# A pre-norm transformer block on one core: the key block that two query tiles share is weighed with split products, and head and tail are reordered

## The chip, the cores and the metric

The kernel runs on one core of a Trainium2 chip. The metric is the device time of one execution in microseconds, the median of the runs shown. TensorE (PE) does the matrix products and is the only writer of the eight PSUM banks; VectorE (DVE) and ScalarE (ACT) read and write SBUF and PSUM; GpSimd (POOL) reads and writes SBUF only here; SyncE (SP) issues all the DMAs. Each engine works through its own instructions in order, and they meet at semaphores.

## The reference

A transformer block on x of 1024 tokens by 256, in float32: layernorm without weights, attention with 16 heads of 128 over a window of 128 keys, a residual, layernorm again, a feed-forward of 1024 with ternary weights and an exact gelu, a residual.

```python
q, k, v = split_heads(h @ wq), split_heads(h @ wk), split_heads(h @ wv)
q, k = _apply_rotary(q, cos, sin), _apply_rotary(k, cos, sin)
valid = (k_pos > q_pos - WINDOW) & (k_pos <= q_pos)
attn = softmax(where(valid, einsum('bhqd,bhkd->bhqk', q, k) * scale, neg))
x = x + concat_heads(einsum('bhqk,bhkd->bhqd', attn, v)) @ wo
# then, on layernorm(x), w1q and w2q being weights rounded to -1, 0, 1:
x = x + einsum('bsf,df->bsd', gelu(einsum('bsd,fd->bsf', h, w1q) + b1), w2q) + b2
```

## The kernel before

**Split products.** Most products run in a one-pass format (`F32R`) on operands that are split in two: a high part, which is the value rounded by a copy into that format, and a low part, which is the value minus the high part. A product of two split operands is three passes: hi by lo, lo by hi, hi by hi. The exception is `weigh_v`, which multiplies plain float32 operands; the profile shows each such product as two instructions.

**Tiles and steps.** There are 64 steps, one for each head and each quarter j of the tokens (two query tiles of 128, `t = 2j` and `2j + 1`). A query tile sees two key tiles: its own and the one ahead of it. So step (head, j) has to do with the key tiles 2j - 1, 2j and 2j + 1, and key tile 2j is seen by both query tiles. On TensorE, step n holds `scores(n)` (into bank `SC`), `transpose_probs(n - 1)` (into `PT`), `project(n + 4)` (q or k of a half of the tokens, into `PR`), a fill if there is one, and `weigh_v(n - 1)` (into `OT`). Fills are the projections of v and of the output for quarters of the tokens, `("v", i)` and `("o", i)`, which use the two banks `VO` in turn; steps 2 to 6 have none. `bank_free` waits until the fill before in the same bank has been read. The last eight steps belong to the last two heads and interleave them.

**The way of a step.** DVE `merge(n)` overlays the two masked halves of the scores and takes the negative maximum; ACT `exps(n)` does the exponentials with sums; DVE `inverse_sum(n)` the reciprocals; ACT `scale_probs(n)`; PE transposes; DVE `mask_pt(n - 1)` writes `probsT`, [128, i, b, 128] for query tile i and key tile b (0: the one ahead, 1: its own); PE `weigh_v(n - 1)`; ACT `ot_hi` and DVE `ot_lo` split its result out of `OT`, and the next `weigh_v` waits for that.

**Rotary.** For each projected chunk m, DVE multiplies by sine (`times_sin`) and by cosine (`times_cos`); SP's `swap(m)` sends the sine product through a DMA that swaps the halves of the partitions; `rotate(m)` adds (L949, on POOL; the first two on DVE at L735); ACT's `rothi(m)` (L589) and `rotlo(m)` (L954 on POOL) split it. POOL also makes the low parts of the weights: `qklo` (L936), `vlo` (L940), `olo` (L944), and the first half of the ternary rounding, `below` (L961), in every second step from 25 to 39; the second half, `ternary` (L796), is DVE's, and both `ternary`'s inputs and its output are in SBUF. In POOL's loop over n the order is `rotlo(n + 2)`, `rotate(n + 3)`, then low parts of weights and `below` where they fall.

**Head and tail.** The head normalises x, transposes it, and does the first projections; the order of each engine's instructions there is written out by hand. The tail takes the steps after 60 into the second layernorm (`tile_stats`, `moments`, `normalise`), whose first half starts when half of the outputs have been added to `xres` (`add_out`, L778), and then the feed-forward (`ffn1` L488, gelu, `ghi` and `glo` for the split, `ffn2` L507).

## Time and profile before

| what | value |
|---|---|
| median of 3 runs | 361.02 us (360.62 to 361.49) |
| the profiled execution's own time | 360.54 us |
| its span | 358.8 us |
| mean granted TensorE clock | 0.99 |
| PE, DVE, ACT, POOL busy | 340.5, 263.8, 208.1, 223.5 us |
| DMA packets, volume | 29025, 31.25 MB |

The span runs from the first to the last instruction of the profiled execution. Busy is the time in which an engine has at least one instruction at work; a PE that is busy throughout is not at its peak, as the ends of its products are modelled and overlap the next one. Times from start to start say more for PE. In the rows below, columns are start us, duration us, engine, line, operation, output<-inputs with buffer numbers left out, shape, count, and in brackets the idle time ahead of it and what ended it.

### The profile page before, as it was taken

Reading aid. Unit: us, or ns where it says so; the run is one execution under the profiler, and the core shown is the slowest. Engines: PE = TensorE matmul, PEld = TensorE weight load, DVE = VectorE, ACT = ScalarE, POOL = GpSimd, SP = SyncE. Lnnn points to the kernel's source line nnn. Section 1 sums busy time; section 2 is a strip of 40 time slices with the busy share of each in tenths; the row PEclk is TensorE's granted clock in tenths of the full one; section 3 lists DMA queues with packets and bytes.
Section 4 is the critical chain, followed back from the end, with each engine's and each line's share of the span. In section 5 each row is a group of like instructions: output and inputs, shape, how many; then the busy total and the mean of one; then the engine's idle time right before and its main releaser. Section 6 shows DMA issues by size and latency. Waiting matters only on the chain.

```text
span 358.8 us, 6923 instructions
## 1 busy us (share of the span) xinstructions
PE 340.5 (95%) x2410; PEld 315.1 (88%) x2410; DVE 263.8 (74%) x607; ACT 208.1 (58%) x626; POOL 223.5 (62%) x182
## 2 busy tenths in 40 slices
PE   7849999999999999999999999999999999898996
PEld 6738778999999999999999999999999999877986
DVE  4874777668766886788788986787678766788681
ACT  2243676677777556655665566556665666365180
POOL 2326778667767678799879987585867656231300
PEclk9997999999999999999999999999999999999999
DMA  7734466543333333333333333333322231000001
GB/s 220 188 95 114 117 164 197 130 102 78 92 83 86 80 84 84 88 81 89 88 90 88 90 88 90 90 89 90 88 61 58 61 88 31 0 3 0 31 29 58
DMA packets 29025, 31.25 MB, mean 87 GB/s; under 512 B 3392, under 2 KB 20288, under 8 KB 28992
## 3 DMA queue, kind: packets, MB, share of 16 engines
q1 hardware_dynamic: 28992, 30.82, 33.7%
q8 instruction: 19, 0.31, 0.4%
q14 instruction: 14, 0.11, 0.1%
HBM read 12.98 MB, written 1.05 MB: 39 GB/s over the span
## 4 chain that ended last, share of the span: by engine, by line
PE 84%; DVE 9%; POOL 2%; issue 2%; DMA 1%; ACT 1%; DVEq 0%; SPq 0%; POOLq 0%
PE PR L385 22%; PE OT L460 15%; PE VO L400 13%; PE SC L435 12%; PE VO L417 11%; PE PT L446 3%; PE PR L488 2%; PE SC L488 2%; PE VO L507 1%; DVE probsT L765 1%; PE SC L507 1%; DVE stats L690 1%; DVE SC L751 1%; DVE gT_lo L807 1%; DVE gT_lo L772 1%
## 5 line engine op out<-in xcount | busy, mean ns | idle before, releaser
L954 POOL TENSOR_TENSOR gT_lo<-turn,gT_hi 128x512 fp32r<-128x512 f32 x62 | 81.7, 1318 | 42.9 <-ACT gT_hi L589 42.7
L949 POOL TENSOR_TENSOR turn<-turn,swapped 128x512 f32<-128x512 f32 x62 | 80.2, 1293 | 38.2 <-DMA swapped<-by_sin 37.9
L594 ACT ACTIVATE probs<-SC,negmax 128x128 f32<-128x128 f32 x128 | 45.8, 363 | 61.9 <-DVE negmax L754 61.9
L460 PE MATMUL OT<-probsT,v_sb 128*128 128x128 f32 x480 | 64.6, 276 | 3.1 <-DVE gT_lo L772 2.7
L601 ACT ACTIVATE probs<-probs,rinv 128x128 f32<-128x128 f32 x128 | 44.5, 395 | 38.2 <-DVE rinv L759 38.2
L460 PEld LDWEIGHTS OT<-probsT,v_sb 128*128 128x128 f32 x480 | 58.9, 191 | 6.0 <-DVE probsT L765 6.0
L385 PE MATMUL PR<-xT_hi,qk_lo 128*128 128x512 f32 x128 | 56.2, 439 | 5.1 <-POOL qk_lo L936 3.7
L751 DVE COPY_PREDICATED SC<-in_prev_sb,SC 128x256 f32<-128x256 int32 x48 | 20.6, 428 | 45.7 <-PE SC L435 45.5
L385 PE MATMUL PR<-xT_hi,qk_hi 128*128 128x512 f32 x128 | 51.0, 398 | 0.0
L385 PE MATMUL PR<-xT_lo,qk_hi 128*128 128x512 f32 x128 | 50.4, 394 | 0.0
L765 DVE TENSOR_TENSOR probsT<-PT,mask_sb 128x512 f32<-128x512 f32 x64 | 43.6, 681 | 1.2 <-PE PT L446 1.2
L589 ACT CAST gT_hi<-turn 128x512 fp32r<-128x512 f32 x64 | 38.9, 607 | 8.5 <-POOL turn L949 7.6
L435 PE MATMUL SC<-gT_hi,gT_lo 128*128 128x256 f32 (+1 forms) x128 | 41.1, 321 | 0.4 <-DVE gT_lo L740 0.4
L400 PE MATMUL VO<-v_lo,xT_hi 128*128 128x256 f32 x128 | 36.7, 287 | 1.0 <-POOL v_lo L940 1.0
L417 PE MATMUL VO<-o_lo,gT_hi 128*128 128x256 f32 x128 | 36.3, 284 | 1.0 <-DVE xres L778 1.0
L400 PE MATMUL VO<-v_hi,xT_hi 128*128 128x256 f32 x128 | 36.6, 286 | 0.0
L400 PE MATMUL VO<-v_hi,xT_lo 128*128 128x256 f32 x128 | 36.5, 285 | 0.0
L417 PE MATMUL VO<-o_hi,gT_hi 128*128 128x256 f32 x128 | 36.0, 282 | 0.0
L435 PE MATMUL SC<-gT_lo,gT_hi 128*128 128x256 f32 (+1 forms) x128 | 36.0, 281 | 0.0
L435 PE MATMUL SC<-gT_hi 128*128 128x256 f32 (+1 forms) x128 | 35.9, 281 | 0.0
L417 PE MATMUL VO<-o_hi,gT_lo 128*128 128x256 f32 x128 | 35.9, 281 | 0.0
L385 PEld LDWEIGHTS PR<-xT_hi,qk_lo 128*128 128x128 f32 x128 | 24.3, 190 | 8.5 <-POOL qk_lo L936 3.9
(114 smaller groups left out, 839.1 us busy)
## 6 DMA issues: line engine op xcount, KB each, us to landing
swapped<-by_sin SPq DMA_DIRECT2D x128, 128.0 KB, 2.3
qk_raw<-in_wq SPq DMA_DIRECT2D x16, 128.0 KB, 2.6
qk_raw<-in_wk SPq DMA_DIRECT2D x16, 128.0 KB, 2.4
v_raw<-in_wv SPq DMA_DIRECT2D x8, 256.0 KB, 3.1
o_raw<-in_wo SPq DMA_DIRECT2D x8, 256.0 KB, 2.9
xres<-in_x SPq DMA_DIRECT2D x4, 256.0 KB, 3.2
w_raw<-in_w1t SPq DMA_DIRECT2D x4, 256.0 KB, 3.0
w_raw<-in_w2t SPq DMA_DIRECT2D x4, 256.0 KB, 3.0
```

Source lines behind the costliest of these rows:

```text
L385: last = mm(PR[m % 2][:], wt[:, c % 2, kd], xt[:, kd, half_of(c)], start=(n == 0), stop=(n == 3 * KD - 1))
L400: last = mm(VO[v % 2][:, i * 256:(i + 1) * 256], xt[:, kd, t * P:(t + 1) * P], wt[:, kd], start=(n == 0), stop=(n == 3 * KD - 1))
L417: last = mm(VO[w % 2][:, i * 256:(i + 1) * 256], ot[:, t * P:(t + 1) * P], wt[:, a], start=(n == 0), stop=(n == 5))
L435: last = mm(SC[n % 2][:, o0:(i + 1) * 256], q[:, t * P:(t + 1) * P], k[:, k0 * P:(t + 1) * P], start=(p_ == 0), stop=(p_ == 2))
L460: last = mm(OT[:, i * P:(i + 1) * P], v_sb[:, t - 1 + b, a * HD:(a + 1) * HD], probsT[:, i, b], start=(b == b0), stop=(b == 1))
L589: copy(rot_hi(head, c % 2)[:, half_of(c)], turn[m % 4][:]).then_inc(rothi_done, 1)
L594: nc.scalar.activation(probs[n % 2][:, i], SC[n % 2][:, i * 256 + P:(i + 1) * 256], ACT.Exp, bias=negmax[:, n % 2, i:i + 1], accum_out=row ...
L601: last = nc.scalar.activation(probs[n % 2][:, i], probs[n % 2][:, i], ACT.Copy, scale=rinv[:, n % 2, i:i + 1])
L751: nc.vector.copy_predicated(sc[:, :, 1], in_prev_sb[:].unsqueeze(1).broadcast_to([P, 2, P]), sc[:, :, 0]).then_inc(merged, 1)
L765: tt(probsT[:], PT[:, 0:256].rearrange("p (i q) -> p i q", i=2).unsqueeze(2).broadcast_to([P, 2, 2, P]), mask_sb[:].unsqueeze(1).broadcast ...
L949: tt(turn[m % 4][:], turn[m % 4][:], swapped[m % 2][:], ALU.add).then_inc(rot_done, 1)
L954: tt(rot_lo(head, c % 2)[:, half_of(c)], turn[m % 4][:], rot_hi(head, c % 2)[:, half_of(c)].bitcast(F32), ALU.subtract).then_inc(rotlo_don ...
```

## The change

Three things change together. (1) v is kept in three tensors: the odd key tiles as float32 (`v_odd`), the even ones split (`v_even_hi`, `v_even_lo`). `probsT` for the shared even key tile, 256 adjacent columns, is split by ACT (`pt_hi`) and POOL (`pt_lo`) into `both_hi` and `both_lo`, and `weigh_v` does it with three 256-column `F32R` products in place of two float32 products of 128 columns. The products of the odd tiles stay. `copy_v` becomes two copies, and DVE gets `v_low`. (2) Steps 2 to 5 weigh into the `VO` banks that the fills leave free then. (3) The order of the head and of the tail changes on all five engines; on DVE `moments(1, 0)` moves to the start and `normalise(1, 0)` to the middle of step 62, `times_sin(3)` and `times_cos(3)` behind `merge(0)`, and on PE `fill(n)` now stands behind `transpose_x(1, 0)` in the last step.

```diff
@@ tensors
-        v_sb = sb("v_sb", [P, NT, 2 * HD])
+        both_hi = sb("both_hi", [P, 2 * P], F32R)
+        both_lo = sb("both_lo", [P, 2 * P], F32R)
+        v_odd = sb("v_odd", [P, NT // 2, 2 * HD])
+        v_even_hi = sb("v_even_hi", [P, NT // 2, 2 * HD], F32R)
+        v_even_lo = sb("v_even_lo", [P, NT // 2, 2 * HD], F32R)
...
+        def ot_bank(n):
+            return VO[n % 2] if 2 <= n <= 5 else OT
@@ sync, head
+            load_head(1)
             load_table(1, cos_sb)
-            load_head(1)
-            swap(0)
             sp.dma_start(in_prev_sb[:], in_prev).then_inc(mask_in, 16)
             sp.dma_start(mask_sb[:].rearrange("p b q -> p (b q)"), mask_t).then_inc(mask_in, 16)
+            swap(0)
             swap(1)
-            swap(2)
             sp.wait_ge(qklo_done, 1)
             load_head(2)
+            swap(2)
             swap(3)
@@ tensor
-                    pe.wait_ge(*((v_copied, user[1] + 1) if user[0] == "v" else (wo_added, o_at[user[1]] + 1)))
+                    pe.wait_ge(*((v_split, user[1] + 1) if user[0] == "v" else (wo_added, o_at[user[1]] + 1)))
...
+                if v in (4, 5):
+                    pe.wait_ge(otlo_done, v + 1)
                 bank_free("v", v)
@@ weigh_v
-                pe.wait_ge(pt_masked, n + 1)
-                pe.wait_ge(v_copied, 4 * (head // 2) + j + 1)
-                if n > 0:
-                    pe.wait_ge(otlo_done, n)
-                for i in range(2):
-                    t = 2 * j + i
-                    b0 = 1 if t == 0 else 0
-                    for b in range(b0, 2):
-                        last = mm(OT[:, i * P:(i + 1) * P], v_sb[:, t - 1 + b, a * HD:(a + 1) * HD],
-                                  probsT[:, i, b], start=(b == b0), stop=(b == 1))
+                hs = slice(a * HD, (a + 1) * HD)
+                pe.wait_ge(v_split, 4 * (head // 2) + j + 1)
+                if n in (2, 3):
+                    bank_free("v", n + 2)
+                elif n > 0:
+                    pe.wait_ge(otlo_done, {4: 3, 5: 4, 6: 2}.get(n, n))
+                pe.wait_ge(both_hi_done, n + 1)
+                mm(ot_bank(n)[:, 0:256], v_even_hi[:, j, hs], both_hi[:], start=True, stop=False)
+                mm(ot_bank(n)[:, 0:256], v_even_lo[:, j, hs], both_hi[:], start=False, stop=False)
+                if j > 0:
+                    mm(ot_bank(n)[:, 0:P], v_odd[:, j - 1, hs], probsT[:, 0, 0], start=False, stop=False)
+                mm(ot_bank(n)[:, P:256], v_odd[:, j, hs], probsT[:, 1, 1], start=False, stop=False)
+                pe.wait_ge(both_lo_done, n + 1)
+                last = mm(ot_bank(n)[:, 0:256], v_even_hi[:, j, hs], both_lo[:], start=False, stop=True)
                 last.then_inc(pv_done, 1)
@@ tensor, order
-            project(3)
             for n in range(STEPS):
                 scores(n)
+                if n == 0:
+                    project(3)
+                    fill(0)
...
-                fill(n)
                 if n == STEPS - 1:
                     transpose_x(1, 0)
                 if n > 0:
+                    fill(n)
                     weigh_v(n - 1)
@@ scalar
-                copy(v_sb[:, 2 * c:2 * c + 2], VO[v % 2][:].rearrange("p (t n) -> p t n", t=2)).then_inc(v_copied, 1)
+                copy(v_even_hi[:, c], VO[v % 2][:, 0:256])
+                copy(v_odd[:, c], VO[v % 2][:, 256:512]).then_inc(v_copied, 1)
+
+            def pt_hi(n):
+                act.wait_ge(pt_masked, n + 1)
+                copy(both_hi[:], probsT[:].rearrange("p i b q -> p (i b q)")[:, P:3 * P]).then_inc(both_hi_done, 1)
...
+            qkhi(1)
             copy_v(0)
             xt_hi(0, 1)
+            rothi(0)
+            rothi(1)
             copy_v(1)
-            rothi(0)
-            qkhi(1)
-            rothi(1)
-            rothi(2)
...
+                if n == STEPS - 1:
+                    xt_hi(1, 0)
                 exps(n)
                 if n == STEPS - 1:
-                    xt_hi(1, 0)
+                    pt_hi(n - 1)
                     ot_hi(n - 1)
                     nc.scalar.preload_act_table(ACT.Gelu)
                 if n > 0:
+                    if n < STEPS - 1:
+                        pt_hi(n - 1)
...
                 scale_probs(n)
+                if n == 0:
+                    rothi(2)
...
                 if k == 1:
+                    pt_hi(STEPS - 1)
                     ot_hi(STEPS - 1)
@@ vector
+            def v_low(v):
+                c = v % 4
+                dve.wait_ge(v_copied, v + 1)
+                tt(v_even_lo[:, c], VO[v % 2][:, 0:256], v_even_hi[:, c].bitcast(F32), ALU.subtract).then_inc(v_split, 1)
...
-            normalise(0, 1)
             times_sin(1)
             times_cos(1)
+            normalise(0, 1)
             rotate(0)
+            rotate(1)
             xt_lo(0, 1)
             rotlo(0)
-            rotate(1)
-            dve.wait_ge(sin_in[1], 32)
-            times_sin(2)
             rotlo(1)
-            dve.wait_ge(cos_in[1], 16)
-            times_cos(2)
+            v_low(0)
+            v_low(1)
...
+            dve.wait_ge(sin_in[1], 32)
+            times_sin(2)
+            dve.wait_ge(cos_in[1], 16)
+            times_cos(2)
@@ vector, steps
-                if n >= LP + 4:
-                    for kind, w in fills(n - 1):
-                        if kind == "o" and w != 4 * PAIRS - 3 and w != 4 * PAIRS - 4:
-                            add_out(w)
...
-                if 0 < n < LP + 4:
+                if 0 < n <= LP + 4:
                     for kind, w in fills(n - 1):
-                        if kind == "o":
-                            add_out(w)
+                        (add_out if kind == "o" else v_low)(w)
+                if n == LP + 4:
+                    add_out(4 * PAIRS - 7)
...
+                if n == STEPS - 2:
+                    add_out(4 * PAIRS - 6)
@@ vector, behind the steps
             add_out(4 * PAIRS - 2)
+            ghi(2)
+            glo(2)
+            glo(3)
             tile_stats(1, 4)
             tile_stats(1, 5)
-            ghi(2)
-            glo(2)
             add_out(4 * PAIRS - 1)
             tile_stats(1, 6)
             tile_stats(1, 7)
             moments(1, 1)
-            glo(3)
@@ gpsimd
+            def pt_lo(n):
+                pool.wait_ge(both_hi_done, n + 1)
+                tt(both_lo[:], probsT[:].rearrange("p i b q -> p (i b q)")[:, P:3 * P], both_hi[:].bitcast(F32),
+                   ALU.subtract).then_inc(both_lo_done, 1)
...
+            vlo(0)
             rsqrt(0, 1)
-            vlo(0)
             pool.wait_ge(rot_done, 2)
+            qklo(1)
             rotate(2)
-            qklo(1)
             pool.wait_ge(rotlo_done, 2)
             for n in range(STEPS - 2):
                 p, s = n // 8, n % 8
                 rotlo(n + 2)
                 if n + 3 < CHUNKS:
                     rotate(n + 3)
+                if n > 0:
+                    pt_lo(n - 1)
...
             rsqrt(1, 0)
+            pt_lo(STEPS - 3)
+            pt_lo(STEPS - 2)
+            pt_lo(STEPS - 1)
```

## Rows read from the trace of the kernel before

**Rows 1.** the page, part 1: busy us, share, instructions
```profile
PE 340.5 (95%) x2410; PEld 315.1 (88%) x2410; DVE 263.8 (74%) x607; ACT 208.1 (58%) x626; POOL 223.5 (62%) x182
```

**Rows 2.** windows by stage: length, busy by engine, clock, DMA share, GB/s
```profile
36.70:60.40 23.70, 21.68 (x145) 18.52 (x144) 18.31 (x43) 15.88 (x53) 19.02 (x15) 1.00 0.58 157
60.40:298.60 238.20, 238.20 (x1746) 224.68 (x1744) 181.89 (x414) 153.31 (x487) 180.30 (x138) 1.00 0.35 87
...
160.00:200.00 40.00, 40.00 (x294) 37.74 (x294) 33.58 (x73) 24.94 (x78) 35.62 (x26) 1.00 0.35 87
```

**Rows 3.** timeline of PE in one step: start, duration, line, what
```profile
142.94 0.36 PE L435 MATMUL SC<-gT_hi,gT_lo 128*128 128x256 f32 x1
...
146.77 1.06 PE L460 MATMUL OT<-probsT,v_sb 128*128 128x128 f32 x8
147.58 0.36 PE L435 MATMUL SC<-gT_hi,gT_lo 128*128 128x256 f32 x1
147.78 0.28 PE L435 MATMUL SC<-gT_lo,gT_hi 128*128 128x256 f32 x1
147.90 0.28 PE L435 MATMUL SC<-gT_hi 128*128 128x256 f32 x1
```

**Rows 4.** timeline of DVE and ACT in that step
```profile
149.38 0.68 DVE L765 TENSOR_TENSOR probsT<-PT,mask_sb 128x512 f32<-128x512 f32 x1
...
150.31 0.68 DVE L719 TENSOR_TENSOR by_sin<-PR,sin_sb 128x512 f32<-128x512 f32 x1
...
150.10 0.20 ACT L594 ACTIVATION_READ_ACCUMULATOR probs<-SC,negmax 128x1 f32 x1
```

**Rows 5.** timeline of POOL around that step; brackets: idle before, and releaser
```profile
144.83 1.30 POOL L949 TENSOR_TENSOR turn<-turn,swapped 128x512 f32<-128x512 f32 x1 [0.23 <-DMA swapped<-by_sin]
146.08 1.29 POOL L936 TENSOR_TENSOR qk_lo<-qk_raw,qk_hi 128x512 fp32r<-128x512 f32 x1
147.73 1.34 POOL L954 TENSOR_TENSOR gT_lo<-turn,gT_hi 128x512 fp32r<-128x512 f32 x1 [0.36 <-ACT gT_hi L589]
150.45 1.29 POOL L949 TENSOR_TENSOR turn<-turn,swapped 128x512 f32<-128x512 f32 x1 [1.37 <-DMA swapped<-by_sin]
151.72 1.55 POOL L961 TENSOR_SCALAR w_sb<-w_raw,thr 128x512 fp32r<-128x512 f32 x1
```

**Rows 6.** durations by shape: instructions of 256 columns on POOL and ACT
```profile
L999 POOL TENSOR_TENSOR xres<-xres,b_sb x8: 719/726/737, 314.7 to 334.4; 128x256 f32<-128x256 f32 x8
...
L613 ACT CAST gT_hi<-OT 128x256 fp32r<-128x256 f32 x53 | 19.3, 365 | 3.0 <-PE OT L460 1.9
```

**Rows 7.** timeline of POOL: first and last of the eight late swaps
```profile
68.19 1.28 POOL L949 TENSOR_TENSOR turn<-turn,swapped 128x512 f32<-128x512 f32 x1 [1.65 <-DMA swapped<-by_sin]
...
283.47 1.29 POOL L949 TENSOR_TENSOR turn<-turn,swapped 128x512 f32<-128x512 f32 x1 [1.53 <-DMA swapped<-by_sin]
```

**Rows 8.** DMA view, 248.2 to 250 us, then the page, part 6
```profile
q8 instruction: 1, 0.02, 5.4%
...
swapped<-by_sin SPq DMA_DIRECT2D x1, 128.0 KB, 3.7
...
swapped<-by_sin SPq DMA_DIRECT2D x128, 128.0 KB, 2.3
```

**Rows 9.** timelines of the head: POOL, then PE
```profile
24.87 1.26 POOL L949 TENSOR_TENSOR turn<-turn,swapped 128x512 f32<-128x512 f32 x1 [10.95 <-DMA swapped<-by_sin]
...
27.40 0.80 PE L385 MATMUL PR<-xT_hi,qk_lo 128*128 128x512 f32 x1 [3.71 <-POOL qk_lo L936]
```

**Rows 10.** timelines of the tail: PE, then DVE
```profile
305.99 0.35 PE L417 MATMUL VO<-o_lo,gT_hi 128*128 128x256 f32 x1 [0.97 <-DVE xres L778]
...
324.42 0.69 DVE L778 TENSOR_TENSOR xres<-VO,xres 128x512 f32<-128x512 f32 x1 [0.77 <-PE VO L417]
```

**Rows 11.** timeline of DVE and POOL, a ternary pass beside a POOL instruction
```profile
183.57 1.66 DVE L796 SCALAR_TENSOR_TENSOR w_sb<-w_raw,thr,w_sb 128x512 fp32r<-128x512 f32 x1
...
184.64 1.74 POOL L936 TENSOR_TENSOR qk_lo<-qk_raw,qk_hi 128x512 fp32r<-128x512 f32 x1
```

16 lines of the change are left out of this document (10 added, 6 removed).

## The prediction

> **What bounds the kernel now.** I read the page first. TensorE is busy 340.5 of 358.8 us and no other engine over 74% [rows 1]. The windows by stage show where that is true: from 60.4 to 298.6 us TensorE is never idle, while in the head and in the six steps 2 to 7 (36.7 to 60.4 us) it is idle for 2.0 us [rows 2]. So in the long stretch, which holds steps 8 to 59, a step costs what TensorE's instructions cost, and any other engine is free as long as it is in time. The second thing to see is that GpSimd is not far from full: 35.62 of 40 us from 160 to 200 us [rows 2]. The third is how a step fits together, which the timelines of the step that begins at 147.58 us show [rows 3 to 5]. Counted from the first scores product: mask ends at 2.48, the last exp read at 2.72, the product by sine at 3.41, and its `weigh_v` begins at about 3.8 (146.77 in the step that began at 142.94). GpSimd does `rotlo`, then waits for the swap of halves, then `rotate`.
>
> **The product itself.** Before, the shared key block costs two F32 products of 128 columns, each two passes. From the first of eight passes (146.77) to the second scores product (147.78) is 1.01 us, less 0.12 for the first scores product: 0.89, or 0.111 a pass [rows 3]. A 256-column product starts 0.12 after the one ahead of it [rows 3]. Removed: 4 x 0.111 = 0.445. Added: 3 x 0.12 = 0.36. Saved: 0.085 a step, in the 52 steps of the full stretch 4.4 us. The bounds: zero if a new product costs 0.148 (the switch between the two kinds is inside the weighing now), and 5.4 us if it counted in all 64 steps.
> The Trainium skill, TensorE: Matmul & The Clock Gate, section "Back-to-back issue gap", gives about 81 ns for a sustained 128-column product with its weight load and 262 cycles (109 ns) for 256 columns. By that, estimated from its figures, four passes would cost 0.324 and three products 0.327, the saving would be nil and the time 4.4 us higher. This case's trace has 0.111 and 0.12 instead, so I give that rule no chance.
>
> **The split of the weights.** ScalarE gets `pt_hi`, 256 columns, 0.365 by the nearest row [rows 6]. It runs after exps, so from 2.72 to about 3.1 of the step, before TensorE wants it at 3.8: hidden in a full step. In steps 2 to 6, which have no fill, TensorE is there at 3.8 - 12 x 0.12 = 2.4 and waits for it until 3.1; the wait for the output bank, now gone, hid most of that, so I count 0.1 to 0.2 a step. Behind it on ScalarE stand the copies of v and the scaling, which waits for VectorE until 3.5 anyway. The second copy of v (+0.15) and `v_low` on VectorE (about 0.4, in the slot where `add_out` stands in the other steps) are hidden by the same idle time: nothing (if not, 0.3 of `rothi`, which GpSimd waits for).
> GpSimd gets `pt_lo`: 0.726 for the same shape [rows 6], taken as 0.70, since a 512-column one of 1.29 is 0.04 shorter from start to start. It is behind `rotlo` and `rotate` in an in-order queue. In a smooth step `rotate` runs from 1.89 to 3.19 (144.83 to 146.13 in the step of 142.94 [rows 3, 5]), `pt_lo` then ends at 3.9, and the last product of `weigh_v` could start at 3.8 + 2 x 0.12 + 4 x 0.111 = 4.5. The slack is 0.6 us. That is the number that decides this change.
>
> **Late swaps.** The slack is less than what swaps are late by. Usually GpSimd sits idle 0.23 us before `rotate`; eight times in the long stretch it is 1.37 us or more, the first and the last at 68.19 and 283.47 us [rows 7], 12.63 us in all. The DMA view says why: in such a window an instruction fetch of 16 KB on queue 8 runs beside the swap, which takes 3.7 us to land and not 2.3 [rows 8]. Today nothing on TensorE waits for it. In the new kernel `pt_lo` stands behind it, and every one stops the last product: 12.63 - 8 x (0.23 + 0.6) = 6.0 us. Example: `rotate` at 150.45 ends at 151.74 [rows 5], `pt_lo` at 152.44, wanted at 151.41 + 0.68 = 152.09. Bounds: 0 if the fetches fall between swaps, and 12.63 - 8 x 0.6 = 7.8 if the 0.23 is not there to be used.
>
> **GpSimd full.** In steps 25 to 41 every second step has a `below` of 1.55 and every other one a 1.29 instruction [rows 5]. Two steps then hold 4 x 1.27 + 2 x 0.70 + 1.53 + 1.27 = 9.28 against 2 x 4.55 = 9.10 of TensorE. Once the slack is used (after three pairs), the rest costs 0.18 a pair, so about 1 us; with `pt_lo` at 0.65 or 0.75 I get 0.9 to 2.6 for the stretch. I take 1.3, near the row's 0.70.
> Sum of steps 8 to 59: -4.4 + 6.0 + 1.3 = +2.9 us.
>
> **The head.** Now `qk_lo` of head 1 stands behind a `rotate` that waits 10.95 us for a swap, and `project(4)` waits 3.71 us for it, after which the products run at half clock (0.80 for the first) [rows 9]. The new order puts `qklo(1)` before that, `load_head(1)` before a table, `vlo(0)` before `rsqrt`, and `scores(0)` before `project(3)`. Walking the queues in the new order, I get `scores(0)` near 19.9 us and `project(4)` near 23.4 instead of 27.4. But `weigh_v(0)` then needs `rothi(3)`, exps(1), `pt_hi`, and on GpSimd `rotlo(3)`, `rotate(4)` and `pt_lo(0)`, one behind the other: it ends near 33.6, so step 2 starts near 33.8 and not 36.7 [rows 2]: -2.9. The masks' DMAs that now stand ahead of `swap(0)` are issued while SP would wait for sine anyway: nothing (their transfer, at most 1 us late for rotate(0)).
> In steps 2 to 7 the weighing no longer waits for the output bank, which cost 2.0 us in all [rows 2], but a loop over two steps binds: product by sine 3.4 after scores, the swap 2.9 to 3.5 later (issue 0.6 and landing 2.3 [rows 8], more with the loads of w beside it), `rotate` 1.3, `pt_lo` 0.7, last product 0.15: 8.45 to 9.05 for two steps, and a 1.27 `qklo` or `vlo` in every second one. Six steps take 25.5 to 26.6 instead of 23.7 us [rows 2]: +1.8 to +2.9, taken +2.4. Head and early steps together: -0.5 (from -1.2 to +0.5).
>
> **The tail.** `o29` waits 0.97 us for an add [rows 10], which now stands a step earlier: gone. The low part `glo(3)` comes before two statistics, so the eighth feed-forward product, which waits for it, comes sooner. But VectorE works without a gap from the add at 324.42 [rows 10] on, and that sets the second half; its work is the same in sum. The add moves by the weighing of the last step, which now needs two gelus, `pt_hi` and `pt_lo` ahead. I get -0.3, and +1.6 if step 60 meets a late swap again, as it does here. I take +0.3.
>
> Total: -0.5 + 2.9 + 0.3 = +2.7 us. Against the profiled execution's own 360.54 (its span of 358.8 and 1.7 around it) that is 363.2; the median of the runs is 0.48 above it, so I say **363.7 us**.
>
> **Rivals.** (1) *The slack holds*: the stop at `pt_lo` is shorter than worked out, and the pure TensorE saving shows: -0.5 - 4.4 + 0.9 - 0.3 = -4.3, 356.7 us; with a third of the stalls left 358.7. For it: the phase of the fetches against the steps is chance, and the new kernel may meet fewer. Against it: the swap is in flight for 2.9 of 4.6 us, and an in-order queue leaves no way around. It decides once the late swaps cost under 3.3 us in sum, 0.41 each and not 0.75. Chance 0.27. (2) *The clock falls again*: TensorE is nearly idle from about 29.6 to 33.6 us in the new head, as it is for 3.7 us today before it drops. Two early steps at half clock: +2.2, 365.9. Chance 0.10. (3) *GpSimd is held by VectorE*: beside the ternary pass of 1.66 us a GpSimd instruction took 1.74 and not 1.29 [rows 11]. If a fuller GpSimd meets all eight, 8 x 0.45 = 3.6: 367.3. The Trainium skill, SBUF — State Buffer, section "Who interferes with whom", says that a VectorE instruction with two SBUF inputs contends with GpSimd's reads; these rows agree. Chance 0.05. (4) Gains and stalls cancel, within 0.2% (0.7 us, about what a measurement of this kernel can tell from no change): 0.08. The forecast has 0.50; its own range is 361.9 to 365.5.
>
> Faster 0.27, same 0.08, slower 0.65. The range goes from 357.5 (rival 1 with a few stalls left) to 367.0 (rival 2 with its margin, nearly all of 3).
>
> **What would show it.** In the profile after: the five or seven passes of the weighing take 0.80 and not 0.89; TensorE has idle time ahead of the last product, released by `both_lo` on GpSimd, some ten times of 0.3 to 1.3 us between 60 and 300 us, each behind a swap that landed late; GpSimd near 268 us busy; step 2 begins near 34 us. I am wrong if that wait is rare or under 3 us in sum.

## The result: 3.7% slower, and the profile after

The changed kernel takes 373.94 us (median of 4 runs, 372.80 to 376.30) against 360.82 in the runs of before made beside it: a ratio of 1.0374, interval 1.0318 to 1.0429. The prediction was 363.7 with a range to 367.0: the direction was right, the size five times too small. The profiled execution took 374.14 us, with a span of 372.2. Medians below are of all runs of a kernel and ratios of its fast runs alone; this matters in e5, e7 and e9, where slow runs are among them, and whose fast runs have medians of 360.82, 363.24 and 359.06 us.

First the page of the kernel after: part 1 (busy time) and part 4 (the chain that ended last, by engine); below them part 4 of the page of before.

```profile
PE 344.2 (92%) x2346; PEld 314.3 (84%) x2346; DVE 277.8 (75%) x639; ACT 227.7 (61%) x722; POOL 269.0 (72%) x246
...
PE 44%; POOL 22%; DVE 12%; DMA 10%; issue 6%; ACT 3%; SPq 2%; DVEq 0%; POOLq 0%
```

```profile
PE 84%; DVE 9%; POOL 2%; issue 2%; DMA 1%; ACT 1%; DVEq 0%; SPq 0%; POOLq 0%
```

TensorE was 95% of the span before [rows 1] and is 92% now. The second line says more: the chain that ended last ran through TensorE for 84% of the span before, and now for only 44%; GpSimd has 22% of it and not 2%, VectorE 12%, and DMA 10%. A kernel that was bound by one engine has become one that is bound by a ring of four. No engine's busy share would tell this: GpSimd is at 72%.

The windows by stage of the kernel after (length, busy by engine, clock, DMA share, GB/s), cut at the first scores products of steps 2, 8 and 60; the rows of before are in [rows 2]:

```profile
0.00:35.03 35.03, 26.97 (x160) 23.50 (x160) 22.92 (x60) 13.37 (x33) 13.75 (x18) 0.97 0.64 172
35.03:63.21 28.18, 24.02 (x137) 20.29 (x137) 18.71 (x44) 17.27 (x60) 22.77 (x21) 0.91 0.43 114
63.21:309.07 245.86, 238.79 (x1692) 221.50 (x1691) 194.54 (x442) 169.03 (x567) 216.75 (x190) 1.00 0.34 84
309.07:372.16 63.09, 54.37 (x363) 49.01 (x361) 41.64 (x93) 28.05 (x66) 15.76 (x19) 0.96 0.07 22
```

Step 2 starts 1.7 us earlier than before, step 8 starts 2.8 later, steps 8 to 59 take 245.9 us in place of 238.2, and the rest 63.1 in place of 60.2. That is +2.8, +7.7 and +2.9, together the 13.4 by which the span grew. In the third row TensorE is busy 7 us less than the window is long, where it had no idle time at all.

What TensorE waits for, in the view of waits over the whole span (in total, how often, the longest; lines are left out at the mark and at the end):

```profile
PE OT L479 <- POOL both_lo L997: 8.2, 10, 1.5
PE OT L473 <- ACT both_hi L633: 4.3, 5, 1.7
...
PE VO L473 <- ACT both_hi L633: 2.4, 4, 0.7
PE VO L479 <- POOL both_lo L997: 1.7, 3, 0.7
```

The first line is the wait that the prediction had named: the last product, for the low part from GpSimd. Between 60 and 310 us it is 6.7 us, nine times. Short waits show in part or not at all, since a product is drawn 0.16 us and more longer than its distance to the next. Two steps in close-up: in step 26 the swap lands in time, in step 32 it lands late. First GpSimd in step 26, which begins at 147.50 us, then GpSimd, VectorE and TensorE in step 32, which begins at 176.25:

```profile
149.79 1.30 POOL L987 TENSOR_TENSOR turn<-turn,swapped 128x512 f32<-128x512 f32 x1
151.05 0.74 POOL L997 TENSOR_TENSOR both_lo<-probsT,both_hi 128x256 fp32r<-128x256 f32 x1
```

```profile
179.90 1.27 POOL L987 TENSOR_TENSOR turn<-turn,swapped 128x512 f32<-128x512 f32 x1 [1.12 <-DMA swapped<-by_sin]
...
180.53 1.20 DVE L832 SCALAR_TENSOR_TENSOR w_sb<-w_raw,thr,w_sb 128x512 fp32r<-128x512 f32 x1
181.14 1.17 POOL L997 TENSOR_TENSOR both_lo<-probsT,both_hi 128x256 fp32r<-128x256 f32 x1
...
182.37 0.38 PE L479 MATMUL OT<-both_lo,v_even_hi 128*128 128x256 f32 x1 [1.54 <-POOL both_lo L997]
```

The sum `rotate` starts 3.65 us into the step and not 2.2 to 2.6, as in the steps beside it, because it waits for its swap. The low part stands behind it, and is itself stretched from 0.74 to 1.17 us by a VectorE instruction that runs at the same time. TensorE stops for 1.54 us, and the step takes 6.34 us in place of 4.75 (step 32 of e7, where nothing waits for the swap). In each of the seven stretched steps (9, 14, 17, 32, 43, 54 and 58) the DMA view between the start of the step and `rotate` shows the packet of queue 8, the instruction fetch, that [rows 8] showed. The other loads that run beside the swaps aren't the reason: of the 104 swap transfers issued in steps 8 to 59 of this kernel, 75 had no packet of an instruction queue beside them and landed 2.16 to 2.37 us after issue, 45 of these beside another load; all that took more than 2.37 us (2.39 to 4.11) had one.

### The profile page after: what moved, and what is told of

It reads as the page before. It is cut to its first block, busy times and chain, and to the rows that moved or that the text cites. A ratio compares the mean times of both kernels' runs of the same rounds, so it can differ in the third digit from the quotient of the medians.

```text
span 372.2 us, 6989 instructions
## 1 busy us (share of the span) xinstructions
PE 344.2 (92%) x2346; PEld 314.3 (84%) x2346; DVE 277.8 (75%) x639; ACT 227.7 (61%) x722; POOL 269.0 (72%) x246
## 4 chain that ended last, share of the span: by engine, by line
PE 44%; POOL 22%; DVE 12%; DMA 10%; issue 6%; ACT 3%; SPq 2%; DVEq 0%; POOLq 0%
PE PR L397 10%; POOL turn L987 9%; DMA swapped<-by_sin 9%; PE SC L449 7%; POOL gT_lo L992 6%; PE VO L431 6%; PE VO L414 5%; POOL both_lo L997 4%; DVE probsT L796 2%; PE OT L479 2%; PE PT L460 2%; PE OT L477 2%; DMA v_raw<-in_wv 2%; PE VO L525 1%; PE OT L476 1%
## 5 line engine op out<-in xcount | busy, mean ns | idle before, releaser
L992 POOL TENSOR_TENSOR gT_lo<-turn,gT_hi 128x512 fp32r<-128x512 f32 x62 | 82.3, 1328 | 16.2 <-ACT gT_hi L609 15.8
L997 POOL TENSOR_TENSOR both_lo<-probsT,both_hi 128x256 fp32r<-128x256 f32 x64 | 47.5, 742 | 18.7 <-ACT both_hi L633 18.1
L449 PE MATMUL SC<-gT_hi,gT_lo 128*128 128x256 f32 (+1 forms) x128 | 36.3, 284 | 0.1
L479 PE MATMUL OT<-both_lo,v_even_hi 128*128 128x256 f32 x60 | 22.6, 377 | 8.5 <-POOL both_lo L997 8.2
L397 PEld LDWEIGHTS PR<-xT_hi,qk_hi 128*128 128x128 f32 x128 | 24.3, 190 | 5.7
```

The source lines that it names most:

```text
L397: last = mm(PR[m % 2][:], wt[:, c % 2, kd], xt[:, kd, half_of(c)], start=(n == 0), stop=(n == 3 * KD - 1))
L449: last = mm(SC[n % 2][:, o0:(i + 1) * 256], q[:, t * P:(t + 1) * P], k[:, k0 * P:(t + 1) * P], start=(p_ == 0), stop=(p_ == 2))
L479: last = mm(ot_bank(n)[:, 0:256], v_even_hi[:, j, hs], both_lo[:], start=False, stop=True)
L992: tt(rot_lo(head, c % 2)[:, half_of(c)], turn[m % 4][:], rot_hi(head, c % 2)[:, half_of(c)].bitcast(F32), ALU.subtract).then_inc(rotlo_don ...
L997: tt(both_lo[:], probsT[:].rearrange("p i b q -> p (i b q)")[:, P:3 * P], both_hi[:].bitcast(F32), ALU.subtract).then_inc(both_lo_done, 1)
```

## The experiments

The diffs are cut to the lines that carry the change. Times are medians; "steps 8 to 59" is the time from the first scores product of step 8 to that of step 60, in the profiled execution (before 238.2, after 245.9). What a stage of a single execution shows can differ from the others of its kernel by the clock, so the range of the runs is given where it is wide.

**e1, the orders alone.** The weighing is the old one, from `v_sb`; `pt_hi`, `pt_lo`, `v_low` and the products of the split are gone, the rest of the change stays.

```diff
-                mm(ot_bank(n)[:, 0:256], v_even_hi[:, j, hs], both_hi[:], start=True, stop=False)
...
+                        last = mm(ot_bank(n)[:, i * P:(i + 1) * P], v_sb[:, t - 1 + b, a * HD:(a + 1) * HD],
+                                  probsT[:, i, b], start=(b == b0), stop=(b == 1))
```

> The changed kernel's orders in head and tail and its use of the fill banks in steps 2 to 5, with the old plain F32 weighing from one V buffer (no both_hi, no both_lo, no v_even_lo). Theory 1 (the loss of 8 us in steps 8 to 59 is the in-order low part on GpSimd): those steps come back to the length of before, 238.2 us from the start of step 8 to the start of step 60 within 0.5, and only what the changed kernel lost outside them stays: step 8 starts up to 2.8 us late because the clock still falls to half inside steps 2 to 7, and the tail loses up to 2.9 us. Time 362 to 366 us, expected 364.5. Rival A (the new orders cost the time, the split gives what it promised): 375 us or more, because the split's gain is missing too. Rival B (the orders are harmless and only the split costs): 359 to 361 us.

Measured: 355.38 us, 0.9864 of before (0.9828 to 0.9900), steps 8 to 59 in 238.1. Theory 1 holds for the long stretch, and is wrong on head and tail: the kernel is 9 us faster than expected, none of the 2.8 us by which step 8 was late stays, and the orders gain 5.2. The window from 20 to 41 us is at full clock. So the fall to half clock in the head of the changed kernel isn't the orders' doing; it comes with the split, and there with the wait for the low part (more on this in the part on the head below).

**e2, the split alone.** The orders are those of before, the bank is OT in every step; `pt_hi`, `pt_lo`, `v_low` and the five products are added.

```diff
-                        last = mm(OT[:, i * P:(i + 1) * P], v_sb[:, t - 1 + b, a * HD:(a + 1) * HD], ...
+                mm(OT[:, 0:256], v_even_hi[:, j, hs], both_hi[:], start=True, stop=False)
+                ...
+                if n > 0:
+                    pt_lo(n - 1)
```

> The three 256-column products with high and low parts, all in OT, in the orders of before (low part of the weights still on GpSimd behind rotate). Theory 1: steps 8 to 59 lose the same 7 to 8 us as in the changed kernel, GpSimd is busy near 268 us, and the head is that of before: 367 to 371 us, expected 369. Rival A (orders cost it): near 357 to 359 us, the gain of 0.085 us in each of 52 steps unspoiled. Rival B (split costs everything): 373 to 375 us.

Measured: 375.92 us, 1.0449 of before (1.0388 to 1.0509), steps 8 to 59 in 246.7. The long stretch is as expected (+8.5); the whole is 7 us above what I expected and nearest to rival B, because steps 2 to 7 take 26.4 us in place of 23.7 and the part behind step 60 takes 63.2 in place of 60.2. The split costs 15 us by itself. The orders by themselves gain 5 (e1), but beside the split they give only 2 of the 15 back (375.92 against 373.94): the diff's two parts have opposite signs, and 3 us of the orders' gain are lost when they are put together.

**e3, no low part of the weights.** The third product reads `both_hi` again, GpSimd's instruction is gone, everything else stays.

```diff
-                pe.wait_ge(both_lo_done, n + 1)
-                last = mm(ot_bank(n)[:, 0:256], v_even_hi[:, j, hs], both_lo[:], start=False, stop=True)
+                last = mm(ot_bank(n)[:, 0:256], v_even_hi[:, j, hs], both_hi[:], start=False, stop=True)
```

> The changed kernel with the subtraction that makes both_lo left out; the third product reads both_hi again in its place, so TensorE's work is the same and GpSimd has 64 instructions of 742 ns less. The low part of the weights is left out of the result. Theory 1: steps 8 to 59 fall to 234 to 235 us (52 times 0.085 below before), no step is stretched by a late swap, TensorE waits for no low part; with head and tail as in the changed kernel 361 to 363.5 us, expected 362. Rival (the extra ScalarE and VectorE work of the split, pt_hi and v_low, costs it): 370 us or more.

Measured: 353.88 us, 0.9811 (0.9789 to 0.9833), 8 us below what I expected: besides the long stretch, step 8 starts 4.7 us earlier than in the changed kernel (58.5 us) and the part behind step 60 is 2.5 shorter (60.6). The window of steps 8 to 59 in this kernel:

```profile
58.49:291.84 233.35, 233.35 (x1692) 219.76 (x1691) 189.55 (x442) 168.47 (x567) 181.07 (x138) 1.00 0.36 88
```

TensorE is busy for all of it, and 238.18 - 233.35 = 4.83 us over 52 steps is 0.093 a step: the promised gain of 0.085 is there. The additional work on ScalarE and VectorE costs nothing in this stretch. Everything that the change loses, 20 us against this kernel, hangs on 64 instructions of 0.74 us and the waits for them.

**e4, the low part on VectorE**, behind the reciprocal of the row sums.

```diff
                 inverse_sum(n)
+                if n > 0:
+                    pt_lo(n - 1)      # on VectorE, no more on GpSimd
```

> The changed kernel with the low part of the weights on VectorE, behind the reciprocal of the row sums, instead of on GpSimd. Theory 1 with its part on late swaps: VectorE's order doesn't wait for the swap transfers of the step, so the stretched steps vanish, and GpSimd is back to some 221 us; VectorE gets 64 instructions of about 0.37 us (some 24 us, busy near 301 us), which delays the cosine product by as much each step, beside a TensorE step of 4.5 us. 362 to 367 us, expected 364. Rival (a VectorE that is full in its turn stretches each step by 0.1 us or more): 368 us or more.

Measured: 368.12 us, 1.0197 (1.0160 to 1.0233), steps 8 to 59 in 242.9. A miss: I had given the instruction 0.37 us. The view of this tile shows what it took (duration min/median/max in ns):

```profile
L813 DVE TENSOR_TENSOR both_lo<-probsT,both_hi x64: 401/425/1539, 33.0 to 328.0; 128x256 fp32r<-128x256 f32 x64
```

It takes 0.40 us in some steps and up to 1.54 in others, 0.681 on average. All 31 that took more than 0.45 us overlap a GpSimd instruction; the 20 that overlap none took 0.40 to 0.43.

**e5, the low product behind the next scores.** TensorE asks for the low part about 1 us later.

```diff
             for n in range(STEPS):
                 scores(n)
+                if n > 1:
+                    weigh_low(n - 2)      # wait for both_lo, last product of the step before
```

> The changed kernel, but the product that reads both_lo is issued one scores later: it stands behind scores of the next step instead of at the end of its own (steps 0 to 61), so GpSimd's low part has some 1 us more before TensorE waits for it. Theory 1 (TensorE stops at the last product for both_lo; without it steps 8 to 59 take 233.3 us): every stretch shrinks by up to 1 us, the late swaps cost some 1.5 us together in place of 7, and steps 26 to 41 lose what exceeds TensorE's step, a GpSimd full for 9.3 us and more in two steps of 9.1: 357 to 362 us, expected 360. Rival (mutual blocking and a full GpSimd alone set the rate, whatever the slack): 369 us or more.

Measured: 362.02 us (359.27 to 366.70 in ten runs), 1.0017 (0.9983 to 1.0050), no different from before; expected were 357 to 362. The same GpSimd with the same work, and 12 us less than the changed kernel; the profiled execution is one of 360.82 us:

```profile
57.76:296.11 238.35, 236.68 (x1693) 220.78 (x1692) 192.91 (x442) 173.54 (x567) 216.64 (x191) 1.00 0.35 87
```

Steps 8 to 25 take 81.3 us, 0.5 more than in e3 (80.8): the late swaps are swallowed. Steps 26 to 41 take 76.0 where e3 has 71.8: here 1 us of slack isn't enough. In the head the clock stays at full speed and step 8 starts at 57.76 us in place of 63.21. What sets the runs of this kernel so far apart isn't shown.

**e6, the low part ahead of the sum** in GpSimd's order.

```diff
                 rotlo(n + 2)
+                if n > 0:
+                    pt_lo(n - 1)
                 if n + 3 < CHUNKS:
                     rotate(n + 3)
-                if n > 0:
-                    pt_lo(n - 1)
```

> The changed kernel with both_lo ahead of the sum turn plus swapped in GpSimd's order. Theory 1: a late swap no longer holds the low part, but the low part waits for both_hi at 2.9 us of the step and the sum then starts behind it, so the same GpSimd work is strung one behind the other: rotlo of the next step moves late by some 0.5 to 1 us. The stretched steps vanish, and each step takes what the chain both_hi, both_lo, sum, its high part on ScalarE, its low part needs: 364 to 376 us, expected 369. Rival (only the late swaps matter): 363 to 365 us, 7 to 8 below the changed kernel's.

Measured: 367.92 us, 1.0205 (1.0158 to 1.0253), as expected, and 6 us below the changed kernel. The profiled execution is the slowest of the four (370.70 us) and takes 245.6 us for steps 8 to 59, no less than the changed kernel. In its waits the low part now waits itself for `both_hi` (16.2 us, 21 times, the longest 2.6, from 60 to 306 us), and all of GpSimd's queue with it; single steps of 7.0 and 6.1 us appear. The stretched steps didn't vanish, against what both sides expected. The step of 7.0 us begins at 148.38, and this stands on VectorE:

```profile
148.16 4.20 DVE L832 SCALAR_TENSOR_TENSOR w_sb<-w_raw,thr,w_sb 128x512 fp32r<-128x512 f32 x1
```

The ternary pass, 0.74 us where nothing holds it, takes 4.20. GpSimd has three instructions of 1.3 us back to back beside it (148.01 to 151.81 us), and the pass ends 0.55 after the last of them. The merge, the exps and `both_hi` are late by that, and TensorE waits 2.15 us for `both_hi`. In the step behind it (6.1 us) the clock is at half for 3.4 us and a swap lands after 4.1. So the order that frees the low part from the swap let VectorE wait here instead.

**e7, no wait for the swap.** The sum reads `by_sin`; the transfers run on.

```diff
-                pool.wait_ge(swap_in[m % 2], 32 * (m // 2 + 1))
+                pool.wait_ge(sin_done, m + 1)
                 pool.wait_ge(cos_done, m + 1)
-                tt(turn[m % 4][:], turn[m % 4][:], swapped[m % 2][:], ALU.add).then_inc(rot_done, 1)
+                tt(turn[m % 4][:], turn[m % 4][:], by_sin[m % 2][:], ALU.add).then_inc(rot_done, 1)
```

> The changed kernel with the sum reading by_sin in place of swapped: the swap transfers still run, but only the sine product two steps later waits for them. The half-swap of the rotation is left out of the result. Theory 1: the seven stretched steps (9, 14, 17, 32, 43, 54, 58, together some 7.4 us above an ordinary step) come back to 4.55 us or, in steps 26 to 41, to 4.8, and the loss of steps 26 to 41 stays: steps 8 to 59 take 238 to 240 us, the time is 364 to 368 us. Rival (late swaps only move a wait that GpSimd's load imposes anyway): 370 us or more.

Measured: 363.33 us, 1.0071 (1.0050 to 1.0092), just under what I expected. Steps 8 to 59 take 238.25, 7.6 less than in the changed kernel; the seven stretched steps alone are 7.5 shorter. That is the share of the late swaps. Steps 26 to 41 still take 76.9.

**e8, no ternary pass on VectorE** (a write of one column in its place).

```diff
-                nc.vector.scalar_tensor_tensor(dest, raw, thr[:, i // 4, 0:1], dest.bitcast(F32), ALU.is_gt,
-                                               ALU.subtract).then_inc(tern_done, 1)
+                nc.vector.memset(mean_abs[:, 0:1], 1.0).then_inc(tern_done, 1)
```

> The changed kernel with the eight VectorE instructions that finish the rounding of the weights replaced by a write of one column each; GpSimd's half of them stays, the second half of the rounding is left out of the result. Theory 1 with mutual blocking (rotlo takes 1.75 us instead of 1.30 beside one of them): steps 26 to 41 come down from 78.1 us by 8 times 0.36, the amount by which a pair (9.64) exceeds GpSimd's own work of 9.28, to 75 us, and the late swaps stay: time 370 to 372 us. Rival (it is VectorE's own late mask product that stretches the pairs): down to 73 us, the time 368 to 369. Rival (only the late swaps cost): no change, 374.

Measured: 369.51 us, 1.0261 (1.0227 to 1.0294). Steps 26 to 41 take 73.6 us, with no late swap among them; e7, without late swaps too but with the passes, has 76.9. So the eight passes cost 3.3 us there. Both numbers on record, 75 for the theory and 73 for the rival, were counted down from 78.1, which holds a late swap (step 32) that this run doesn't meet. As differences they were 2.9 and 5.1, so 3.3 is nearer to the theory of mutual blocking. But the edit also takes the passes' own time from VectorE, and how the 3.3 divide between GpSimd held and VectorE late isn't shown. In steps 26 to 41 of e7 six GpSimd instructions are held, by some 0.45 us each; here none is. The rows of the changed kernel show how both lose (VectorE, then GpSimd):

```profile
151.84 1.74 DVE L832 SCALAR_TENSOR_TENSOR w_sb<-w_raw,thr,w_sb 128x512 fp32r<-128x512 f32 x1
```

```profile
151.74 1.30 POOL L974 TENSOR_TENSOR qk_lo<-qk_raw,qk_hi 128x512 fp32r<-128x512 f32 x1
152.98 1.75 POOL L992 TENSOR_TENSOR gT_lo<-turn,gT_hi 128x512 fp32r<-128x512 f32 x1
```

The pass starts 0.1 us into a GpSimd instruction that then ends at 153.04, and ends itself at 153.58. It takes 0.74 to 0.78 us where it isn't held. GpSimd's next one starts at 152.98 and takes 1.75. VectorE is then late with the masked product of the next step (it ends 2.91 us into the step, not 2.40), and with it `pt_hi` and `pt_lo` are.

**e9, GpSimd's low part made and not used.** As e3, but the 64 instructions run, and only the masked product of the next step waits for them.

```diff
                     dve.wait_ge(pv_done, n)
+                    dve.wait_ge(both_lo_done, n)
```

> The changed kernel with GpSimd's 64 low parts still run, but the third product reads both_hi, so TensorE waits for none of them; only the masked product of the next step waits until the low part has been read out. The low part of the weights is left out of the result. Theory 1 (the cost is TensorE's wait in its own step, not GpSimd's load): steps 8 to 24 and 42 to 59 are as without the low part (4.54 us), and only steps 26 to 41, where two steps hold 9.3 to 9.6 us of GpSimd's work beside 9.1 of TensorE's, fall behind by 1 to 4 us: steps 8 to 59 take 234 to 238 us, the time is 354.5 to 359 us, expected 356. Rival (GpSimd's load as such delays the rotation): 365 us or more.

Measured: 359.12 us, 0.9956 (0.9931 to 0.9982), steps 8 to 59 in 237.0: 80.8 for steps 8 to 25 as in e3, and 74.9 for steps 26 to 41 (e3 71.8). The stretch came out as expected, the total just above the range (357.80 to 363.38 in ten runs; the profiled execution is the fastest of them). The same load on GpSimd costs 3.6 us in the long stretch when TensorE doesn't wait in its own step and 12.5 when it does. The load as such is the smaller part.

**e10 and e11, the low part on VectorE with an operand in PSUM**, e11 also with the late product of e5. The masked shared block goes to the free half of bank PT.

```diff
-                tt(probsT[:], PT[:, 0:256]..., mask_sb[:]..., ALU.mult).then_inc(pt_masked, 1)
+                tt(probsT[:], PT[:, 0:256], mask_sb[:, 0:2 * P], ALU.mult)
+                tt(PT[:, 256:512], PT[:, 0:256], mask_sb[:, P:3 * P], ALU.mult).then_inc(pt_masked, 1)
...
-                tt(both_lo[:], probsT[:]..., both_hi[:].bitcast(F32), ALU.subtract)
+                tt(both_lo[:], PT[:, 256:512], both_hi[:].bitcast(F32), ALU.subtract)
```

> The low part of the weights on VectorE, but the masked shared block is written to the free half of bank PT, and both its high and its low part read it there. In the run with the low part on VectorE 64 instructions took 0.40 us when GpSimd was idle and up to 1.54 us beside one of its instructions (mean 681 ns), while those that read a bank kept their time. Theory 1 with mutual blocking: the low part takes 0.40 to 0.45 us always; the masked product becomes two of 256 columns, some 0.8 us together in place of 0.68. VectorE's work falls by some 10 us against the run before, to 303, and steps 8 to 59 to 233.5 to 238 us: the time is 356 to 361 us, expected 358. Rival (VectorE's number of instructions is what costs, wherever they read): 366 us or more.

> The kernel before this one in the list, with the third product behind scores of the next step as well. Both parts of theory 1 together: no product waits for a low part any more, steps 8 to 59 take 233.3 to 235.5 us and no step is above 4.7; head as in the order-only kernel: 353.5 to 358 us, expected 355.5, that is at or a little above the order-only kernel's 355.4. Rival (late low product brings a wait of ScalarE's for the finished bank): 360 us or more.

Measured: e10 359.93 us, 0.9979 (0.9962 to 0.9997), steps 8 to 59 in 237.1; e11 356.18, 0.9881 (0.9854 to 0.9909), 235.9. The tile's line of e10, to be held against that of e4:

```profile
L814 DVE TENSOR_TENSOR both_lo<-PT,both_hi x64: 400/402/425, 32.0 to 319.3; 128x256 fp32r<-128x256 f32 x64
```

None of 64 is held any more, though 49 of them overlap a GpSimd instruction; the two masked products take 0.41 and 0.42. (VectorE writes a PSUM bank here, as `merge` does in every kernel of this document; TensorE isn't the only engine that writes the banks.) VectorE has more instructions than in e4 and the kernel is 8 us faster, 5.8 of it in steps 8 to 59: it wasn't their number. e11 came out as expected in sum, but not in the stretch: it still has a step of 5.9 us at step 20, where TensorE waits 1.03 us for the readout of the sums that set the thresholds.

**e12, the orders alone, all in OT.**

```diff
         def ot_bank(n):
-            return VO[n % 2] if 2 <= n <= 5 else OT
+            return OT
```

> The order-only kernel with steps 2 to 5 weighed into OT as the others, not into the banks of the fills. Theory on the head: the gain of the new orders (355.4 against 360.6 us) comes from TensorE's clock, which stays up in the head because the third projection, the first scores and the fill stand closer together, and not from the banks: 355 to 357 us, clock at full speed from 25 to 33 us. Rival (the extra banks free TensorE in steps 2 to 5 and carry the gain): 358 to 360 us.

Measured: 356.30 us, 0.9881 (0.9849 to 0.9912). The banks of the fills carry little or nothing of the gain (the intervals of e1 and e12 overlap).

**e13, one exchange in the kernel before.**

```diff
-            rotate(2)
             qklo(1)
+            rotate(2)
```

> The kernel before with one exchange: GpSimd makes the low part of head 1's projection weights ahead of the sum turn plus swapped of chunk 2, instead of behind it. In the trace of before TensorE stands 3.71 us until 27.40 for that low part, which could start at 20.5 us (its high part is done) but stands behind the sum, which waits for its swap until 24.87; the clock then falls to half for 6.8 us. Theory 2 (the same in-order wait on GpSimd as in the changed kernel, in the head of before): TensorE goes on at 23.7, the clock stays up or falls later, and the kernel takes 355.5 to 358.5 us, most of what the order-only kernel gained. Rival (something else in the head ends last, the rotation of chunk 3 or the first probabilities): 360 us or more.

Measured: 356.57 us, 0.9879 (0.9859 to 0.9899): 4.1 of the 5.2 us that all the new orders bring, from one exchange of two lines. GpSimd in its head:

```profile
21.58 1.29 POOL L936 TENSOR_TENSOR qk_lo<-qk_raw,qk_hi 128x512 fp32r<-128x512 f32 x1 [7.48 <-DVE turn L735]
25.00 1.29 POOL L949 TENSOR_TENSOR turn<-turn,swapped 128x512 f32<-128x512 f32 x1 [2.13 <-DMA swapped<-by_sin]
```

The low part ends at 22.87 us, where it ended at 27.35 behind the sum that stands at the same place as before (25.00 against 24.87 [rows 9]). The longest wait of TensorE between 22 and 34 us is now 0.94, and the window from 25 to 34 us is at full clock.

**e14, the clock alone.**

```diff
+                if n == 0:
+                    keep_warm(OT, 15)
                 if n + 4 < CHUNKS:
                     project(n + 4)
```

> The kernel before with 15 products of constants, read by nobody, in the 3.71 us that TensorE stands before 27.40 (0.22 us each, 3.3 us together). The wait for the low part stays. Theory of the clock: the 4.5 us of products from 27.40 to 31.94 run at full speed and save 2.2 us: 358 to 359 us. Rival (what follows the gap waits for the rotation anyway, or the clock falls later instead): 360.3 to 361.5 us.

Measured: 358.54 us, 0.9934 (0.9910 to 0.9958), as the theory had it. The products of constants fill the wait, `project(4)` still starts at 27.57, but at full speed, and the kernel gains 2.1 us. So half of e13's gain is the clock, the other half the wait itself.

**e15, the split with both causes taken out.** e11, with the sums of sizes in bank OT.

```diff
-                mm(PT[:, 256:264], mean_ones[:], abs_sum[:]...).then_inc(mean_done, 1)
+                mm(OT[:, 256:264], mean_ones[:], abs_sum[:]...).then_inc(pv_done, 1)
```

> The split with its low part on VectorE from PSUM and the low product behind the next scores, as in the last series, but with the sums of the feed-forward weights' sizes in the free half of bank OT, since that kernel stopped at step 20 for their readout (a step of 5.88 us in place of 4.54). Theory 1: steps 8 to 59 come down from 235.9 to 234.5 us and the time to 354 to 355.5, at or below the order-only kernel's 355.4 (0.9864 of before). Rival (the stall moves to the banks' use): 356 us or more.

Measured: 355.36 us, 0.9843 (0.9800 to 0.9887), the best of the kernels that compute everything, and not to be told from e1 (0.9864). Its long stretch is that of the kernel that makes no low part:

```profile
58.10:291.96 233.86, 233.46 (x1694) 219.94 (x1692) 211.07 (x545) 170.63 (x567) 181.21 (x138) 1.00 0.36 88
```

## Why the prediction was right, and wrong

**Right: the product.** The first product of the weighing in step 26 and the first two of the next scores:

```profile
151.26 0.28 PE L473 MATMUL OT<-both_hi,v_even_hi 128*128 128x256 f32 x1
...
152.07 0.28 PE L449 MATMUL SC<-gT_hi,gT_lo 128*128 128x256 f32 x1
152.19 0.28 PE L449 MATMUL SC<-gT_lo,gT_hi 128*128 128x256 f32 x1
```

Counted as before, from 151.26 to 152.19 less 0.12, the weighing takes 0.81 us where 0.80 was said and 0.89 stood before. e3 shows it as 4.83 us in the long stretch, said 4.4.

**Right in its mechanism, a quarter too small: the late swaps.** "In the new kernel `pt_lo` stands behind it, and every one stops the last product": 6.0 us were said, with eight stops. There are seven in steps 8 to 59, and e7 gives them 7.6 us. My forecast of where to see it, some ten waits of up to 1.3 us between 60 and 300 us, was right too (nine times, up to 1.5).

**Wrong in size: "GpSimd full", 1.3 us.** Steps 26 to 41 lose 76.9 - 71.8 = 5.0 us even without a late swap (e7 against e3). e8 splits them: 3.3 go with the eight ternary passes and 1.8 stay, which is the term as I had meant it. Even that was loosely derived: my pair of 9.28 against 9.10, with the slack spent first, gives 0.9, and neither the 1.3 nor the range of 0.9 to 2.6 follows from it. A pair takes 9.20 us in e8 and 8.98 in e3, so 0.22 are lost in each of eight pairs and the slack takes up none of them. The 3.3 belong to rival 3, priced at 3.6 and given a chance of 0.05. It wasn't a rival at all but a term of the same sum: the rows of before [rows 11] already showed 1.74 for 1.29. What is new isn't how often they meet. In steps 26 to 41 five GpSimd instructions are held in the kernel before, seven in e3, eight in the changed kernel; before and in e3 that costs TensorE nothing, because GpSimd has idle time behind them (65 us of instructions in 73 us before), and in the changed kernel it has none (79 in 78, drawn with small overlaps). The Trainium skill, SBUF — State Buffer, section "Who interferes with whom", says that a VectorE instruction with at most one SBUF input, outside its 2-port modes, doesn't contend with GpSimd, and that one with two contends with a GpSimd instruction that reads SBUF. This case's traces agree: 0.40 to 1.54 us in e4 against 0.40 to 0.43 in e10.

The sum of the long stretch is then -4.8 + 7.6 + 1.8 + 3.3 = +7.9, and the trace has +7.7; said were +2.9.

**Wrong: the head**, "-0.5 us", 3.3 off. The walk through the queues had the parts right (`scores(0)` at 19.9, measured 20.31; step 2 at 33.8, measured 35.03), but not what a nearly idle TensorE means there. These are TensorE and GpSimd in step 1 of the changed kernel:

```profile
32.49 0.35 PE L473 MATMUL OT<-both_hi,v_even_hi 128*128 128x256 f32 x1 [1.68 <-ACT both_hi L633]
34.65 0.58 PE L479 MATMUL OT<-both_lo,v_even_hi 128*128 128x256 f32 x1 [1.47 <-POOL both_lo L997]
```

```profile
31.42 1.27 POOL L992 TENSOR_TENSOR gT_lo<-turn,gT_hi 128x512 fp32r<-128x512 f32 x1 [0.73 <-ACT gT_hi L609]
32.65 1.27 POOL L987 TENSOR_TENSOR turn<-turn,swapped 128x512 f32<-128x512 f32 x1
33.88 0.72 POOL L997 TENSOR_TENSOR both_lo<-probsT,both_hi 128x256 fp32r<-128x256 f32 x1
```

Two waits of 1.68 and 1.47 us with 0.5 us of work between them; then 6.8 us at half clock (1.2 GHz):

```profile
31.00:33.20 2.20, 0.70 (x4) 0.54 (x4) 1.52 (x4) 2.20 (x10) 1.78 (x2) 1.00 0.25 57
33.20:40.00 6.80, 5.35 (x19) 4.77 (x20) 2.40 (x6) 3.44 (x11) 5.27 (x6) 0.50 0.21 59
```

That is rival 2, to which I gave 0.10 and 2.2 us. It too was no alternative to the forecast but a consequence of it: the text had found that TensorE would be nearly idle from 29.6 to 33.6 us. The rest of the head can be divided: step 2 is 1.2 us later than said, and steps 2 to 7 take 28.2 us where 26.1 was said. In e2 and e6 the low part is on GpSimd too and the clock is full in these steps; they take 26.5 and 26.9. So the loop over two steps was about right, and 1.3 to 1.7 us there are the clock. (Three pairs of 8.45 to 9.05 are 25.4 to 27.2 us, not the 25.5 to 26.6 of my text; the value that I took hardly changes.) e5 shortens the second of the two waits to 0.77, its clock doesn't fall, and step 8 starts 5.5 us earlier, by both. e6, e9 and e10 have the first wait and not the second, and their clock doesn't fall there either; in e4, which has the first alone too, it falls for 3.4 us, so the second wait doesn't settle it by itself. Without the split the same orders bring step 8 to 56.73, 3.7 us before the old kernel (e1): that gain is real, e13 shows that one exchange carries it, and the split used it up.

**Wrong: the tail**, "+0.3", measured +2.9. TensorE waits there for `both_hi` four times, 2.6 us together, where before it waited 1.1 for the bank and the mask; and the clock is at half for 3.4 us:

```profile
347.00:349.00 2.00, 2.00 (x13) 2.00 (x12) 0.00 (x0) 0.00 (x0) 0.01 (x1) 0.55 0.00 0
349.00:351.00 2.00, 2.00 (x13) 2.00 (x12) 1.31 (x3) 1.08 (x2) 0.00 (x0) 0.59 0.00 0
```

The fall isn't bound to the split: e1 has one as well, with a tail of 60.8 us, and e12, the same orders in one bank, has none and 59.3. e7 has the waits of the changed kernel for `both_hi`, no fall of the clock, and a tail of 61.5 (e8 too). So 1.5 to 1.6 us of the tail are the clock. The rest can be read from the other tails without a fall: 60.2 before, 59.3 with the new orders alone (e12), 60.6 with the split but no low part (e3), 61.5 with it (e7). The orders give 0.9 us, the high part and its waits cost 1.3, the low part 0.8; these are differences of single executions. Why the clock falls in some executions and not in others after the same two waits of 0.9 and 0.6 us isn't settled.

The step that failed, in one sentence: I added up the stops of a full step and set the blocking and the clock beside them as rivals that exclude the forecast, at 0.05 and 0.10, when both are set off by the very waits and load that the forecast works out. With them in the sum (+3.6 and +2.2, by my own prices) it would have said 369.5. The other 4 to 5 us are terms that were in the sum and too small: the tail by 2.6, the late swaps by 1.6, the head by another 1.1.

The lesson from the other side is in e5: the decisive number, a slack of 0.6 us for an instruction behind a wait that is at times 1.4 us late, could have been turned from 0.6 to 1.6 by moving one product, with no further instruction on any engine. It brings the split back to the time of before (e5), not below it; for that the low part had to leave GpSimd as well (e11, e15).

## What to carry to other kernels

Before an instruction whose result the bounding engine needs in the same step is put behind one that waits for a DMA on an in-order engine, compare the slack with the latest landing in the trace and not with the usual one; if it is less, move the consumer (e5), the producer's engine (e10) or the order (e13; e6 shows an order that moves the wait to another engine). Costs that the forecast's own waits bring about, a fallen clock and an engine held by another, belong in the sum and not among the rivals. When moving an elementwise instruction from GpSimd to VectorE, give it an operand in PSUM, or it will wait for the engine it was to relieve (0.68 us on average here against 0.40). And take apart a diff with two halves: here one was worth -5 us and the other +15, and together they were +13.

## What the runs showed of the hardware

- A VectorE subtraction with both operands in SBUF took 0.40 to 1.54 us (mean 0.681) beside a busy GpSimd; the same with one operand in PSUM took 0.40 to 0.43, all 64 times, 49 of them beside one (e4, e10).
- It goes both ways: a GpSimd instruction of 512 columns behind such a one took 1.75 us in place of 1.30, and one of 256 columns 1.17 in place of 0.74. A ternary pass of 0.74 took 4.20 beside three GpSimd instructions back to back (e6).
- All seven swaps that stretched a step had a packet of the instruction queue in flight beside them. Without one a transfer of a swap landed in 2.16 to 2.37 us, with another load beside it or not; with one it took up to 4.11. In this kernel TensorE pays for code loading through a chain of sine product, transfer, sum and low part.
- After two waits of 1.68 and 1.47 us close together TensorE's clock was at half (1.2 GHz) for 6.8 us in the changed kernel, and after the same two for 3.4 us in e7 and e8. In the tail, after waits of 0.90 and 0.58, it fell for 3.4 us in some kernels and not at all in others. It shows in the spread: the runs of e1 with a mean clock of 0.999 and more took 354.9 and 355.0 us, those at 0.995 took 355.8 and 357.5; those of e15 took 353.5 to 354.1 at 0.999 and more, and 356.6 to 357.9 at 0.989 to 0.995.
